# A Mamba decoder block: B kept with tokens on partitions and spread by float32 transposes, and the skip term made by TensorE in the middle of a job

## The reference

```
u = silu(causal_dwconv(u, cw, cb))                    # 512 channels
dt, Bm, C = split(einsum('bld,ed->ble', u, xp_w))     # 16, 64 and 64 columns
dt = softplus(einsum('blr,dr->bld', dt, dtw) + dtb)
# for each token t, with 64 states for each channel:
h = h * exp(dt_t[:, :, None] * A) + (dt_t * u_t)[:, :, None] * B_t[:, None, :]
y = einsum('bds,bs->bd', h, C_t)
return ys + u * D_skip                                # the skip term
```

## Time and profile before

| What | Value |
|---|---|
| median of 3 runs | 3466.93 us (3465.08 to 3469.7) |
| the profiled execution | 3468.26 us |
| its span in the trace | 3466.5 us |
| VectorE busy | 3132.8 us, 90% |
| ScalarE busy | 2795.2 us, 81% |
| GpSimd busy | 2707.2 us, 78% |
| TensorE busy, matmuls | 2655.7 us, 77% |
| first product of the scan loop starts | 44.08 us |
| gate of the last job starts | 3252.99 us |

### The profile page before, as it was taken

One profiled execution on the slowest core, in us unless ns is written; L12 is line 12 of the kernel. 1 busy time (PEld: TensorE's weight loads), 2 busy tenths in 40 slices (PEclk: granted clock), 3 DMA queues, 4 the chain that ended last, 5 costly groups with the idle time before them and its releaser, 6 DMA issues.

```text
span 3466.5 us, 50869 instructions
## 1 busy us (share of the span) xinstructions
PE 2655.7 (77%) x17556; PEld 2274.8 (66%) x17556; DVE 3132.8 (90%) x2269; ACT 2795.2 (81%) x6418; POOL 2707.2 (78%) x1335
## 2 busy tenths in 40 slices
PE   5767676787777788788787777878878778888876
PEld 3666565666656667677676666767767666777766
DVE  4999999999999999999999999999999999999610
ACT  6979899887989798887888868888797968887422
POOL 5889888887989788787878878787887978877501
PEclk7889998988899899899899988999999879899988
DMA  2242111111111133222242122413323123343486
GB/s 97 86 138 65 46 47 49 52 47 52 47 47 48 48 113 100 81 84 95 73 143 77 68 92 77 140 62 98 122 81 119 50 73 114 99 141 125 136 267 191
DMA packets 148758, 319.64 MB, mean 92 GB/s; under 512 B 25466, under 2 KB 41859, under 8 KB 147988
## 3 DMA queue, kind: packets, MB, share of 16 engines
q1 hardware_dynamic: 144546, 305.60, 26.8%
q0 software_dynamic: 3072, 8.39, 0.7%
q10 hardware_dynamic: 882, 2.38, 0.2%
HBM read 286.42 MB, written 29.88 MB: 91 GB/s over the span
## 4 chain that ended last, share of the span: by engine, by line
issue 32%; DVE 24%; POOL 20%; ACT 12%; PE 11%; DMA 1%; SPq 0%; POOLq 0%; DVEq 0%; ACTq 0%
POOL hC L919 17%; DVE h L1159 11%; DVE psX L1149 10%; ACT dA L1127 5%; ACT xs L1102 2%; PE psY L1422 2%; PE psX L1406 2%; PE psG L1374 2%; PE psX L1374 1%; POOL scratch L832 1%; PE psG L1450 1%; PE psX L1450 1%; DVE gT L1174 1%; POOL gT L842 0%; POOL dtu L855 0%
## 5 line engine op out<-in xcount | busy, mean ns | idle before, releaser
L919 POOL TENSOR_TENSOR hC<-h,cb 128x1024 f32<-128x1024 f32 x1024 | 2405.9, 2366 | 535.0 <-DVE h L1159 526.8
L1159 DVE TENSOR_TENSOR_SCAN h<-dA,psX 128x1024 f32<-128x1024 f32 (+1 forms) x1113 | 2313.6, 2107 | 70.9 <-PE psX L1406 41.9
L1127 ACT ACTIVATE dA<-dt,negA 128x255 f32<-128x255 f32 x4096 | 1717.5, 501 | 124.4 <-DVE h L1159 120.4
L1422 PE MATMUL psY<-ident,hC 128*128 128x128 f32 x8192 | 1186.4, 293 | 61.4 <-DVE gT L1174 41.4
L1422 PEld LDWEIGHTS psY<-ident,hC 128*128 128x128 f32 x8192 | 1041.3, 153 | 96.2 <-DVE gT L1174 44.9
L1406 PE MATMUL psX<-ident,xs 128*128 128x128 f32 x3488 | 537.5, 305 | 300.2 <-ACT xs L1102 150.8
L1149 DVE TENSOR_TENSOR psX<-dtu,psX 128x1024 f32<-128x1024 f32 x588 | 710.5, 1208 | 60.2 <-POOL dtu L855 37.1
L1406 PEld LDWEIGHTS psX<-ident,xs 128*128 128x128 f32 x3488 | 440.3, 156 | 399.7 <-ACT xs L1102 227.4
L1102 ACT ACTIVATE xs<-dtuT,bT 128x512 f32<-128x512 f32 x872 | 579.8, 717 | 9.9 <-PE psX L1406 9.3
L1397 PE MATMUL psX<-bparts,sel 96*128 96x256 bf16 x588 | 172.8, 294 | 238.5 <-DVE h L1159 230.3
L1397 PEld LDWEIGHTS psX<-bparts,sel 96*128 96x128 bf16 x588 | 59.7, 102 | 349.9 <-DVE h L1159 322.0
(11 more groups left out here) (217 smaller groups left out, 1880.1 us busy)
## 6 DMA issues: line engine op xcount, KB each, us to landing
cb<-c_dram SPq DMA_DIRECT2D x256, 512.0 KB
w_up<-in_w_exp SPq DMA_DIRECT2D x198, 256.0 KB
w_down<-in_w_exp SPq DMA_DIRECT2D x198, 256.0 KB
dA<-in_w_exp SPq DMA_DIRECT2D x42, 256.0 KB, 4.2
h<-in_w_exp SPq DMA_DIRECT2D x42, 256.0 KB, 4.4
x_slots<-got SPq DMA_DIRECT2D x16, 512.0 KB, 5.4
xg<-x_slots SPq DMA_DIRECT2D x60, 128.0 KB
y_slots<-yg SPq DMA_DIRECT2D x60, 128.0 KB
```

What stands on the lines that cost most here:

```text
L919: eng.tensor_tensor(hC[i % NHC][:, :, :], h[i % NH][:, :, :], cw.to_broadcast([P, KI, L]), ALU.mult).then_inc(times_c, 1)
L1127: made = eng.activation(dA[j % NA][:, c, 1:L], dt[n % 2][:, c, 1:L], ACT.Exp, scale=negA[:, JOBS[n][0], c, s:s + 1])
L1159: made = eng.tensor_tensor_scan(h[i % NH][:, part, :].rearrange("p c t -> p (c t)"), dA[i % NA][:, part, :].rearrange("p c t -> p (c t)"), ...
L1422: made = eng.matmul(psY[:, tc, c * P:(c + 1) * P], hC[i % NHC][:, c, tc * P:(tc + 1) * P], ident[:, :], start=s == 0 and c == 0, stop=Fals ...
```

## The change

B is now made with tokens on partitions at once: for each half of the tokens u is the stationary operand and w_x the moving one (64 columns), and one ScalarE copy puts it into bT. `spread_b` makes two float32 transposes of one column of bT, broadcast to 128 columns, in the place of the bfloat16 matmul. The tasks `b_hi`, `b_rest`, `b_mid`, `b_rest2`, `b_lo`, `b_turn` and `skip` are gone, with their tiles and semaphores. The tile `diag` holds D on the diagonal of a 128 by 128 matrix for each layer and chunk, made once at the start by eight ScalarE instructions from `ident`. `add_skip` multiplies u by it with float32 matmuls and stands ahead of `sum_states` of step 32 of its job. The gate waits for the last `sum_states`. The weights w_x are loaded in three pieces. The planner counts `sum_states` of step 32 three times SUM and no longer the last one twice.

```diff
-            task("b", n, 0, "PE", 2 * MM, ("silu", n, 0), opens="G"),
-            task("b+", n, 0, "PE", 2 * MM, ("b", n, 0)),
-            task("b", n, 1, "PE", 2 * MM, ("b+", n, 0)),
-            task("b+", n, 1, "PE", 2 * MM, ("b", n, 1)),
-            task("b_hi", n, 0, "ACT", 2 * EVICT, ("b+", n, 1), *((("b_rest", n - 1, 0),) if n else ()), frees=("b", n, 0)),
-            task("b_rest", n, 0, "POOL", 1200, ("b_hi", n, 0)),
-            task("b_mid", n, 0, "ACT", EVICT, ("b_rest", n, 0)),
-            task("b_rest2", n, 0, "POOL", 1200, ("b_mid", n, 0)),
-            task("b_lo", n, 0, "ACT", 2 * EVICT, ("b_rest2", n, 0))]
+            task("b", n, 0, "PE", 8 * TURN, ("silu", n, 0), opens="G"),
+            task("b+", n, 0, "PE", 8 * TURN, ("b", n, 0)),
+            task("bT_copy", n, 0, "ACT", 330, ("b+", n, 0), frees=("b", n, 0))]
...
-                    at["PE"] = sum_end[j] = max(at["PE"], c_end[j]) + SUM * (2 if j % S == S - 1 else 1)
+                    at["PE"] = sum_end[j] = max(at["PE"], c_end[j]) + SUM * (3 if j % S == S // 2 else 1)
...
+            for to, at, many in ((0, 0, HALF), (HALF, 3 * HALF, HALF), (S, 6 * HALF, S + R)):
+                eng.dma_start(w_x[:, :, :, to:to + many], io["w_x"][:, :, :, at:at + many]).then_inc(mamba_in, 16)
...
-                    elif name == "skip":
-                        on.wait_ge(dtu_done, 2 * (n + 1))
-                        for c in range(KI):
-                            made = eng.activation(u[n % 2][:, c, :], u[n % 2][:, c, :], ACT.Identity,
-                                                  scale=dskip[:, JOBS[n][0], c:c + 1])
-                        made.then_inc(skipped, 1)
...
+            on.wait_ge(set_up, SETUP + 1)
+            for l in range(LAYERS):
+                for c in range(KI):
+                    made = eng.activation(diag[:, l, c, :], ident[:, :], ACT.Copy, scale=dskip[:, l, c:c + 1])
+            made.then_inc(diag_made, 1)
...
                 on.wait_ge(silued, n + 1)
+                on.wait_ge(summed, S * (n + 1))
                 for tc in range(KL):
-                    on.wait_ge(y_done, KL * n + tc + 1)
...
-                on.wait_ge(b_lo_done, n + 1)
+                evicted(("b", n, 0))
                 on.wait_ge(scanned, i - 1)
-                eng.matmul(psX[i % 2][:, KI - 1, :], sel[:, s % HALF:s % HALF + 1].to_broadcast([3 * HALF, P]), bparts[n % 2][:, s // HALF, :],
-                           start=True, stop=True).then_inc(x_in, 1)
+                for tc in range(KL):
+                    made = eng.transpose(psX[i % 2][:, KI - 1, tc * P:(tc + 1) * P], bT[n % 2][:, tc, s:s + 1].to_broadcast([P, P]), ident[:, :])
+                made.then_inc(x_in, 1)
...
             def add_skip(n):
-                on.wait_ge(skipped, n + 1)
+                on.wait_ge(diag_made, 1)
+                on.wait_ge(silued, n + 1)
                 for tc in range(KL):
                     for c in range(KI):
-                        made = eng.matmul(psY[:, tc, c * P:(c + 1) * P], u[n % 2][:, c, tc * P:(tc + 1) * P], ident[:, :],
-                                          start=False, stop=True, is_transpose=True, skip_group_check=True)
-                    made.then_inc(y_done, 1)
+                        eng.matmul(psY[:, tc, c * P:(c + 1) * P], u[n % 2][:, c, tc * P:(tc + 1) * P], diag[:, JOBS[n][0], c, :],
+                                   start=False, stop=False, skip_group_check=True)
...
-                        made = product(dst[0:3 * HALF, part * L:(part + 1) * L],
-                                       [(w_x[:, l, c, part * 3 * HALF:(part + 1) * 3 * HALF], u[n % 2][:, c, :])
-                                        for c in (2 * i, 2 * i + 1)], not second, second)
-                        if part == i == 1:
+                        made = product(dst[:, i * S:(i + 1) * S], [(u[n % 2][:, c, i * P:(i + 1) * P], w_x[:, l, c, 0:S]) for c in range(KI)])
+                        if second:
...
-                    if j % S == S - 1:
-                        add_skip(j // S)
```

83 lines of the change are left out of this document (17 added, 66 removed).

## The result

Over seven executions each, the kernel before has a median of 3468.8 us (3465.1 to 3470.4) and the changed kernel one of 3456.4 us (3454.0 to 3462.7). The ratio is 0.9967, 95% interval 0.9955 to 0.9978: 12.4 us faster, where 16 us less and 3451 us (3436 to 3469) were forecast. The time lies in the range and on the forecast side of the 0.2%, but 5 us above the forecast, and the inside of the sum came out differently from what the total suggests.

What follows compares the result with a forecast made beforehand. VectorE was taken to bound the kernel, so the loop could shorten only by its waits; -18.6 + 5 + 2 - 2.5 - 2.9 + 1 = -16.0 us gave 3451 us against the median, range 3436 to 3469 us.

Steps and rivals of the forecast that it cites:

- The main term, -18.6 us: Loop: VectorE's waits behind ScalarE's cuts of B; 14 without softplus go whole, half of the 8 with it.
- the 23.6 us of all waits: Loop: the sum of the 22 VectorE waits behind a ScalarE copy that cuts B; the main term's upper end.
- the rival by which most of them change their owner: Loop: softplus keeps dA late, only 5 us of waits come back; -2.4 us, 3465 us, chance 0.17.
- the sentence that the skip term at the end of a job gives nothing back: Job ends: removing it gains nothing in 15 jobs; the gate did not wait for its 0.9 us of idle TensorE.
- the waits at the boundaries stay: Job boundaries: waits from TensorE's lower clock after the gate, 0.94 us at one, were taken as unchanged.
- The mid-job skip term: Middle of a job: eight float32 matmuls make TensorE 1.5 us late in one job in twelve or so; +2 us.
- The longer spread: Plain steps: two float32 transposes take 0.11 us more, exposed at 0.08 us in some 60 cases; +5 us.
- The head: Before the first product: cheaper records for b and no b_rest2 ahead of dtu; -2.5 us.
- The tail: From the last gate: gate 0.5 us earlier, transposes at once behind it 2.4 us; -2.9 us, with +1 us for clock.
- The third rival: Tail: thinned-out TensorE work halves the clock of the last row's matmuls, 5.7 us more; 3456 us, chance 0.10.
- My +1 us: Tail: TensorE, with fewer matmuls around, may be granted less clock; +1 us, ends 0 and 5.7.
- The signs I had named: New profile: predicted waits, busy times, first product and tail length that would show the forecast right or wrong.

Runs made afterwards that it cites:

- e_before_warm: The kernel before, with 20 extra identity transposes before the first sum of a job at seven boundaries and 181 in the tail: 3463.6 us.
- e_hole: The changed kernel with eight identity transposes where the old skip term had its eight, at eight of fifteen job ends: 3450.8 us.
- e_warm_tail: The changed kernel with 181 unread identity transposes behind ten groups of the last row's matmuls: 3448.7 us.
- e_edge_tail: The changed kernel with 20 identity transposes before the first sum of a job at nine boundaries and 181 in the tail: 3428.7 us.
- e_warm_share14: e_edge_tail with 14 turned steps in place of 12 in each run of the last ten jobs: 3415.3 us.

## Why the prediction was right, and where it was not

**The main term, -18.6 us, held.** The waits behind the cuts of B on ScalarE are what the change removes. Tenths 5 to 7 lost 17.2 us; with the cuts alone left out they lost 19.1 us; with the clock held up in both kernels they differ by 16.3 us. These three readings lie around the 18.6 us and below the 23.6 us of all waits, so some waits stayed, and the rival by which most of them change their owner fails. The named waits of the whole loop without the cuts fell by 20.5 us.

**The step that failed** is the sentence that the skip term at the end of a job gives nothing back, since the gate did not wait for it, and took 0.9 us of an idle TensorE; with it the sentence that the waits at the boundaries stay. For time on the path the first was right. But taking these transposes away made the boundaries dearer, and the sum had no term for that. The kernel with the old skip term is 10 us faster (3446.1 us, against 3456.0 beside it). The cost is not tied to where the new skip term stands, since leaving it out changes nothing. About half of it, 5.7 us, came back with eight useless transposes in the old place at eight boundaries, and at these the first sum then ran at the lower clock throughout once in the place of 4 to 7 times. So for this half the clock is shown as the cause. For the rest it is likely and not shown: seven boundaries were not filled, and 4 us of the 10 are VectorE's own work in another order. In the profiled executions the term is +0.3 to +8 us of waits in tenth 1, +7.6 in the one of the changed kernel. The earlier trace rows showed the lower clock behind the gate; I used it as a price and did not ask what the removed work did to it. That row alone could not have told, as the clock was low there with the old transposes in place.

**Terms mis-sized.** The mid-job skip term: +2 us forecast, nothing measured. The longer spread: +5 us forecast, with twice its growth again costing 5 us; 2 to 3 us is likely. These two were too high by 4 to 5 us and the missing one was 7.6 in that execution; that the loop agreed to 0.2 us is luck.

**The head**, -2.5 us, did not come in the profiled execution, and this too goes with the clock. The timeline of the changed kernel has

```profile
34.12 3.51 PE L1327 MATMUL psG<-w_x,u 128*128 128x64 f32 x16
37.56 3.78 PE L1327 MATMUL psG<-cdt,shared 17*128 17x256 f32 x8
```

and that of the kernel with the hole filled, whose head is the same program, has

```profile
31.01 1.90 PE L1327 MATMUL psG<-w_x,u 128*128 128x64 f32 x16
32.84 1.99 PE L1327 MATMUL psG<-cdt,shared 17*128 17x256 f32 x8
```

with a granted clock of 0.50 and 0.93 in the stretch from 30 to 35 us. b's 16 records take 1.90 us, my lower bound from the 0.12 us of a record (1.95). Of the eleven profiled executions with the new b, five had this faster form and a head of 30.0 to 30.4 us, 2.4 to 2.8 us less than before; the others had 31.2 to 33.0. So the term is right where the clock comes back in time and nearly nothing where it does not. The head of the kernel before is not one number either: the same head took 34.0 us in the profiled execution of e_before_warm.

**The tail**, -1.9 us forecast, was +2.6. Its -2.4 us came: the first transposes follow the last gate at 3246.67 us. The 0.5 us of an earlier gate did not: it stands 6.9 us behind the start of the last scan (before: 6.4), and one expert tile more precedes the last sums. And the clock took more than the 2.4 us back. The third rival, with its 5.7 us, was the better description: holding the clock up gives 7.7 us. My +1 us was the mis-sized term. In the terms of the forecast the outcome, 3456 us, is that rival's number exactly, but not for its reason alone: the boundaries took their part as well, so the agreement is luck.

**The signs I had named.** Scan waits of some 32 us: 33.1. Spread waits of 20 to 27 us: 27.4, at the edge, in 28 cases. No wait over 1 us at steps 35 and 36: the longest that stands in the 12 us behind a skip term is 0.98 us. GpSimd 37 us less: 34.5. ScalarE 77 us less: 63.1; the removed groups are as the earlier trace rows had them, and the rest of the difference is spread over dA, diag and the timing of overlapping instructions, and was not followed up. The first product near 41.6 us: 47.3, 3.0 us of it a later first matmul behind the load of w_in, which was 11.3 to 14.3 us in all the profiles. The tail from the last gate on, at most 213.5 us: 215.6, so by its own sign the forecast was wrong for the tail.

## What to carry to other kernels

Work that stands on nobody's path can still keep an engine's clock up: before pricing the removal of TensorE work at nothing, look at what runs directly behind it, at which granted clock, and whether the next idle time begins there. Look at all such places, in more than one execution: here the first boundary showed 0.2 us and all fifteen together up to 8. Where short rows of matmuls between two waits bound the kernel, some useless transposes into a free bank are a cheap test of this, and here also, with the tail's, a gain of 28 us, more than twice that of the change itself. And a shorter loop is only worth what the order behind it leaves: twice here, with 18 and 27 us, part of the gain turned up again as expert and routing work behind the last scan.

## What the runs showed of the hardware

- At six job boundaries TensorE idled 2.6 to 3.5 us before the first sum behind the gate, and the sum took 1.97 us at 3 to 5 of them in four kernels with idle time further ahead, and at one of them with eight transposes put in there (e_hole, 2.93 or 3.47 us of idling). So the idle time just before does not alone decide the clock; the work before it counts. It does not decide alone either: in the kernel before, with eight transposes in that place and 3.47 us of idling, the first boundary's sum took 1.97 us.
- Transposes that nobody reads hold the clock up too: in the tail the granted clock was 1.00 with them (3247 to 3267 us in e_warm_tail), and 0.73 and 0.50 without (3250 to 3300 us in the changed kernel).
- One program's boundaries differ from one execution to the next. In the profiled pair with the same loop (3191.1 and 3181.7 us) the waits in tenth 1 were 28.2 and 20.9 us, and a sum that took 1.97 us at the 13th boundary in one took 1.10 us in the other, behind the same 2.64 us of idling. The executions of the changed kernel spread over 8.7 us (seven), those of e_edge_tail over 0.9 us (four), but those of e_warm_share14, padded alike, over 6.1 us (five).
